# Signs of the routed rows made one slot later on ScalarE, and VectorE's convolutions ahead of the scores, in the last ten slots of a gated delta layer

## The reference

```python
    x = x + _L0_attn_b_ref(_layernorm(x), ...)     # gated delta
    x = x + _L0_ffn_ref(_layernorm(x), ...)        # routed splines
...
        q = _silu(_dwconv_causal(x @ Wq, conv_q_w, conv_q_b))   # k, v alike
        alpha = sigmoid(x @ Wa + ba); beta = sigmoid(x @ Wb + bb)
        # scan over t:
                err = einsum('bhvk,bhk->bhv', S, kt) - vt
                S = at * S - bt * err * kt
                o = einsum('bhvk,bhk->bhv', S, qt)
        o = (o - mu) * rsqrt(var + 1e-05) * ln_w + ln_b
        o = (o * sigmoid(x @ Wg)) @ Wo
...
            # routed splines, xf = layer-normed rows
            input_sigs = sign(xf)
            cluster_scores = input_sigs @ cluster_sigs.T
            best_cluster = argmax(cluster_scores)
            tile_scores = input_sigs @ tile_sigs.T
            tile_idx = argmax(where(in_cluster, tile_scores, -inf))
```

## Time and profile before

| what | value |
|---|---|
| median of 3 runs | 3161.95 us |
| the profiled execution's own time | 3159.97 us |
| its span | 3158.2 us |
| slots 64 to 73 (from the first `carried` of slot 64, 2759.86, to the end of the last residual, 3073.37) | 313.51 us |
| of it busy: VectorE, TensorE, GpSimd, ScalarE | 258.92, 215.15, 173.11, 157.06 us |
| granted TensorE clock, mean of slots 64, 65, 66, 67, 68 | 0.88, 0.84, 0.84, 0.87, 0.84 |
| the same, slots 69, 70, 71, 72, 73 | 0.97, 0.94, 1.00, 0.87, 0.56 |
| behind them, to the end of the span | 84.83 us |

### The profile page before, as it was taken

The page is one execution under the profiler, slowest core; times in us unless marked ns, Lnnn a source line. Parts: engine busy times, 40 slices in busy tenths (PEclk is TensorE's granted clock), DMA queues, the critical chain, the costliest instruction groups (busy, mean ns, idle before and its releaser), DMA issues.

```text
span 3158.2 us, 65711 instructions
## 1 busy us (share of the span) xinstructions
PE 2652.7 (84%) x21856; PEld 2161.5 (68%) x21872; DVE 2253.1 (71%) x5574; ACT 2146.7 (68%) x5247; POOL 2029.7 (64%) x2171
## 2 busy tenths in 40 slices
PE   6889889646579999999999999999999999877753
PEld 3555555425458788887878888788787888756642
DVE  5777778575457776776767767667677677679876
ACT  4767776424358777878878778788787787755631
POOL 3544554333667778787786877868768787676442
PEclk9999999667789999999999999999999999988975
DMA  2000000014577676776767666676776767633311
GB/s 98 0 0 0 0 0 0 3 55 108 137 188 206 159 203 153 193 195 160 202 155 193 191 172 180 175 190 179 178 185 177 194 162 192 163 84 99 82 28 53
DMA packets 750315, 402.08 MB, mean 127 GB/s; under 512 B 406867, under 2 KB 686163, under 8 KB 749910
## 3 DMA queue, kind: packets, MB, share of 16 engines
q1 hardware_dynamic: 750038, 398.59, 48.4%
HBM read 263.80 MB, written 134.62 MB: 126 GB/s over the span
## 4 chain that ended last, share of the span: by engine, by line
PE 40%; DVE 16%; POOL 15%; issue 14%; ACT 12%; DMA 1%; SPq 1%; POOLq 0%; DVEq 0%; ACTq 0%
PE bank L2051 16%; PE bank L2219 7%; PE bank L2102 4%; ACT acc L1116 3%; POOL outer L877 3%; PE bank L2082 3%; POOL ors L890 3%; POOL prob L776 2%; POOL inv L880 2%; ACT shifted L1114 2%; DVE acc L1646 2%; POOL acc L863 2%; POOL oT L896 2%; PE bank L2167 2%; DVE ostat L1705 2%
## 5 line engine op out<-in xcount | busy, mean ns | idle before, releaser
L863 POOL TENSOR_TENSOR acc<-acc,shifted 128x510 f32<-128x510 f32 x384 | 585.0, 1524 | 460.6 <-DVE acc L1646 458.7
L1646 DVE SCALAR_TENSOR_TENSOR acc<-bank,conv_w,acc 128x254 f32<-128x254 f32 (+1 forms) x1536 | 630.1, 471 | 190.1 <-ACT acc L1116 189.5
L2051 PE MATMUL bank<-x_k,w_kq 128*128 128x256 f32 x2048 | 507.8, 398 | 25.3 <-DMA x_k<-xT_scratch 25.3
L1114 ACT ACTIVATE shifted<-bank,conv_w 128x255 f32<-128x255 f32 x768 | 366.0, 476 | 136.7 <-issue 66.9
L2051 PEld LDWEIGHTS bank<-x_k,w_kq 128*128 128x128 f32 x2048 | 387.4, 196 | 90.0 <-DMA x_k<-xT_scratch 15.2
L1116 ACT ACTIVATE acc<-bank,conv_b,conv_w 128x256 f32<-128x256 f32 x768 | 438.5, 571 | 0.0
L776 POOL TENSOR_TENSOR prob<-prob,rinv 128x512 f32<-128x512 f32 x192 | 201.8, 1054 | 266.3 <-DVE rinv L1442 266.1
L2219 PE MATMUL bank<-w_o,oT 128*128 128x256 f32 x1024 | 249.4, 389 | 80.8 <-POOL oT L896 79.2
L880 POOL TENSOR_TENSOR inv<-inv,outer 128x30 f32<-128x30 f32 (+14 forms) x480 | 285.8, 595 | 37.6
L877 POOL TENSOR_TENSOR outer<-inv 128x30 f32<-128x30 f32 (+14 forms) x480 | 264.8, 552 | 35.9 <-DMA inv<-D_scratch 7.9
L2219 PEld LDWEIGHTS bank<-w_o,oT 128*128 128x128 f32 x1024 | 188.4, 193 | 122.8 <-issue 99.3
(11 more groups left out here) (243 smaller groups left out, 5849.8 us busy)
## 6 DMA issues: line engine op xcount, KB each, us to landing
abc<-decay_scratch SPq DMA_DIRECT2D x64, 512.0 KB, 5.2
MTm<-M_scratch SPq DMA_DIRECT2D x128, 256.0 KB, 3.4
kqm<-q_scratch SPq DMA_DIRECT2D x64, 512.0 KB, 4.9
knm<-k_scratch SPq DMA_DIRECT2D x64, 258.0 KB, 4.0
x_k<-xT_scratch SPq DMA_DIRECT2D x64, 256.0 KB, 2.9
q_scratch<-kq SPq DMA_DIRECT2D x128, 128.0 KB, 3.1
q_scratch<-kq SPq DMA_DIRECT2D x64, 256.0 KB, 3.6
D_scratch<-LM SPq DMA_DIRECT2D x256, 64.0 KB
```

The lines of the kernel that those rows point to most:

```text
L863: pool.tensor_tensor(dst, dst, shifted[:, u % 2, :, 1:], ALU.add).then_inc(Z["sumk" if u < 4 else "sumv"], 1)
L1114: act.activation(shifted[:, u % 2, i % 2, 1:], pj[:, 0:SEQ - 1], ACT.Copy, scale=conv_w[:, kind, bass.ds(head, 1), TAPS - 2:TAPS - 1].rear ...
L1646: dve.scalar_tensor_tensor(out=acc[:, kind, i, t:], in0=pj[:, 0:SEQ - t], scalar=wcol, in1=acc[:, kind, i, t:], op0=ALU.mult, op1=ALU.add) ...
L2051: mm = pe.matmul(dst[:, i * SEQ:(i + 1) * SEQ], w[:, k, head * DK:(head + 1) * DK], x[:, k, :], start=(k == 0), stop=(k == CT - 1))
```

## The change

ScalarE makes the signs of a slot's unit in the next slot, behind `joined("x")` and ahead of `gate(0)`, and no longer as the last thing of the slot itself. Those of slot 73 are made behind the last slot together with those of 74, which is where they stood. VectorE's list runs conv(4), conv(5), weighted, scores, second_out, spread instead of conv(4), scores, conv(5), second_out, weighted, spread. Nothing is added or removed, and no wait is edited.

```diff
@@ block.scalar, slot(s)
-                rt = drained(s)
+                old = drained(s - 1)
...
                     if joining(s):
                         joined("x")
+                    if old:
+                        signs(tiles1, old[0], old[2])
                     if h is not None:
                         gate(0)
...
                     if h is not None:
                         from_state()
-                    if rt:
-                        signs(tiles1, rt[0], rt[2])
...
-            g, b, w = drained(STEPS + LAG_N)
-            signs(tiles1, g, w)
+            for s in (STEPS + LAG_N - 1, STEPS + LAG_N):
+                g, b, w = drained(s)
+                signs(tiles1, g, w)
@@ block.vector, slot(s)
                     if f is not None:
-                        conv(4)
-                    routed(3)
-                    if f is not None:
-                        conv(5)
-                    if n is not None:
-                        second_out()
+                        conv(4), conv(5)
                     if h is not None:
                         weighted()
+                    routed(3)
                     if n is not None:
-                        spread(), moments_of_out()
+                        second_out(), spread(), moments_of_out()
```

## The result

The changed kernel takes 3153.93 us (median of 9 runs, 3148.21 to 3158.05), the kernel before 3161.36 beside it (9 runs, 3158.54 to 3165.29): a ratio of 0.9974, with a 95% interval of 0.9964 to 0.9984. In microseconds that is 7.4 gained, 5 to 11 by the interval. The forecast was 3154.5, faster by 7.4 us.

A forecast was written before the change was run, and what follows sets the result against it. VectorE was taken to bound the next `carried` in slots 64 to 73 once `upper` is free. 4.67 + 0.65 + 4.3 - 0.3 + 0.6 - 2.0 - 0.5 - 0.25 + 0.2 = 7.4 us gained: 3154.5, range 3150 to 3160.5.

The forecast's parts named there:

- tails: From a slot's `spread` to the next `carried`: VectorE idles there vanish, 4.67 us in slots 65 to 68, 0.65 in 69.
- wide fronts: From `carried` to `spread` in slots 66 to 69: 10.0 us each, 4.3 gained, less 0.3 in slot 66.
- The step that TensorE gets ahead: Turn of slot 68 to 69: with `upper` free earlier, TensorE leads VectorE by about 3.6 us, so `carried` needn't wait.
- GpSimd was taken at 0.2 a slot: Wide slots: VectorE operations waiting for GpSimd's scales cost 0.2 us a slot, out of a possible 0 to 1.0.
- the tail of slots 64 and 69 to 71: Between `spread` and the next `carried`: no loss; +0.65 us in slot 69, and `spread` 0.6 earlier in slot 64.
- narrow fronts: From `carried` to `spread` in slots 70 and 71: 1.0 us lost in each, -2.0 together, bounds -1.1 and -2.2.
- Slower: Rival, chance 0.07: TensorE not ahead, signs on the chain in every slot, wide fronts 13.1, 11 us lost, 3173.
- Held back: Rival, chance 0.18: sign product waits for GpSimd's power or `add_shifted(5)`, TensorE cools; gain 3.2 us, 3158.8.
- Nothing: Rival, chance 0.08: something hidden, `project_out` or a load, bounds the wide slots' tails; 2.7 us gained, 3159.
- Slot 73 and what follows: Slot 73 loses about 0.25 us and gains 0.2 at its start; what follows is in the same order.
- the forecast case: Outcome with a gain of 5 to 9 us, chance 0.53; about five sevenths of it measurably faster.
- faster: Sign of the whole-kernel time: less than 3155.6 us, given chance 0.58 as 0.14 + 0.44.

The follow-up runs named there:

- signs_only: Changed kernel, but with VectorE's order of the kernel before; only ScalarE's signs are moved: 3172.43 us, ratio 1.0037 to the kernel before.
- order_only: Changed kernel, but with the signs left last in ScalarE's slot; only VectorE's list is new: 3172.83 us, ratio 1.0028 to the kernel before.
- wide_state_early: Changed kernel, but slots 64 and 70 to 73 in the order of before, except `weighted` ahead of `second_out`: 3151.57 us timed, ratio 0.9965 to the kernel before.
- state_late: Changed kernel, but with `weighted` behind `second_out` in every slot: 3156.81 us in one run, 3160.52 for the kernel before beside it.
- wide_only: Changed kernel, but slots 64 and 70 to 73 keep the order of the kernel before: 3153.78 us, ratio 0.9973 to the kernel before.
- early_signs: Against `wide_only`, signs of the wide units stand behind `tap(5)`, ahead of `lower`: 3151.09 us, ratio 0.997 to the kernel before.

## Why the prediction was right, and where it was off

**The bound and the tails held.** The idles ahead of `carried` were what the tail could give. Slots 67 and 68 gave 1.10 and 1.90 (forecast 1.15 and 1.93), slot 66 0.20 instead of 0.60: its power starts 2.87 us behind `spread` where it was 2.59, and 0.3 had been taken off for that. Slot 65 gave 1.48 (0.99): its front grew by 2.28 and its tail shrank by 3.76, GpSimd setting the point in between.

**The wide fronts held**: 10.12, 10.14, 9.73 and 9.69 for a forecast of 10.0, worth 4.66 us in slots 66 to 69 against 4.3 less 0.3. The step that TensorE gets ahead is shown three times: by the rows of the turn, by `signs_only`, which has it and the short tails, and by `order_only`, which lacks both. GpSimd was taken at 0.2 a slot. In slots 66 to 69 it is GpSimd that pays. Slot 68 after the change:

```profile
2903.36 1.72 POOL L744 TENSOR_TENSOR frs<-fvar,half_neg 128x4 f32<-128x4 f32 x1
2905.16 1.11 POOL L749 TENSOR_TENSOR fvar<-frs 128x4 f32<-128x4 f32 x1
```

against 1.02 and 0.20 alone: the power runs beside `weighted` (2903.53, 0.68 long) and the next scale beside the sign product (2904.99), and both VectorE operations keep their own length. The scale began 0.17 behind the product and waited, as the forecast had it. The Trainium skill (SBUF — State Buffer, "SBUF: two separate sides") has an exclusive lock, by which the later of the two waits; the scale agrees. The power doesn't: by its row it began 0.17 ahead of `weighted` and is longer by `weighted`'s length all the same, in slots 66, 67 and 68 alike. Why GpSimd loses there, no run shows; that the rows of GpSimd start too early is possible.

**The term that failed is the tail of slots 64 and 69 to 71.** The forecast put nothing there ("TensorE's own `second_out` needs some 1.2 ... and hides") except +0.65 in slot 69 and +0.6 in slot 64; it never asked what `weighted` ahead sets off on TensorE. The state came earlier, nobody needed it earlier, and the idle that had been in pieces became one piece ahead of `outT`, after which the granted clock was 0.52. Slot 64's front won 0.31 and its tail lost 0.92: -0.61 instead of +0.6. That one is not sure to come: `order_only` and the second execution of `wide_state_early` have the same order there and an idle of 3.73 ahead of `outT`, where the changed kernel has 3.72, and still an `outT` of 1.11 and 1.09 and tails of 18.86. Slot 69's tail is 0.46 longer instead of 0.65 shorter; `state_late` and `signs_only`, with `weighted` late, have the 18.9 that the forecast worked out. Slots 70 and 71 lose 0.66 and 0.64. `second_rhs` waits 1.69 longer there; about 0.94 of it comes back, since VectorE used to wait that long for `project_out` later in slot 70 and now doesn't. In all 3.3 us of the forecast's sum. In slots 66 to 68 the clock fell too, at no price:

```profile
2915.24 1.97 PE L2206 MATMUL bank<-ident,o 128*128 128x128 f32 x8 [5.66 <-DVE o L1722]
```

This is `outT` of slot 68, 1.04 long before the change. But `second_rhs` waits for TensorE in none of these three slots, as VectorE's parts for four tiles lie ahead of it, and the tails came out as forecast.

**The narrow fronts were right in kind, not in size.** Slot 70 paid 0.11, slot 71 1.59, for -1.0 in each slot. In slot 70 a premise was wrong: TensorE is ahead there too, `carried` starts without the idle of 1.04 that it had, and TT's copy ends at C + 6.17 instead of C + 6.71. In slot 71 `carried` waits as before, and the collision with `add_shifted(5)` that was priced "up to 0.5" costs 0.94:

```profile
2998.17 1.26 POOL L863 TENSOR_TENSOR acc<-acc,shifted 128x510 f32<-128x510 f32 x1
...
2998.35 1.63 DVE L1361 TENSOR_TENSOR sgn<-sgn,sl_sign 128x512 f32<-128x512 f32 x1 [0.98 <-ACT sgn L991]
```

In slot 71 the product starts 0.18 behind the addition and takes 1.63; in slot 70 it takes 0.69:

```profile
2968.10 0.69 DVE L1361 TENSOR_TENSOR sgn<-sgn,sl_sign 128x512 f32<-128x512 f32 x1 [0.98 <-ACT sgn L991]
```

Without it slot 71's front would have paid 0.65, where the forecast's own sum had 0.6. The price depends on how much of the addition is left: in `state_late` it starts 0.73 ahead of the product in slots 70 and 71, and the product takes 1.09 and 1.08. Slot 72 took +0.52 for +0.3.

**The rivals.** "Slower" did not happen; `order_only`, where TensorE isn't ahead either, shows wide fronts as long as it feared, by another path. "Held back" happened in one slot of nine, as the product in slot 71. "Nothing" fell: no load and no `project_out` stands behind the idles of the wide slots.

**The total.** The drain of the traces gained 5.4 us, the medians say 7.4 and, repeated, 6.3, with an interval of 3 to 11. So the traces bear out less than the forecast's sum, and that the median hit it to 0.6 us is partly luck. Slot 73 and what follows was 0.69 shorter instead of 0.25 longer. That is TensorE's clock in `project_out` of slot 73, before and after:

```profile
3066.68 5.96 PE L2219 MATMUL bank<-w_o,oT 128*128 128x256 f32 x16 [1.60 <-POOL oT L896]
```

```profile
3064.99 5.31 PE L2216 MATMUL bank<-w_o,oT 128*128 128x256 f32 x16 [1.61 <-POOL oT L896]
```

The granted clock is 0.61 in the first and 0.69 in the second. In the twelve profiles the stretch from slot 73 on is 107.0 to 107.5 us where this product takes 5.1 to 5.4, and 108.1 to 108.6 where it takes 6.0 to 6.2; the two executions of `wide_state_early`, one kernel, are one of each. So this gain too is outside the forecast's mechanism.

**A slip in the chances.** Five sevenths of the forecast case's 0.53 are 0.38, not 0.44, so that "faster" had 0.52 by the forecast's own terms.

## What to carry to other kernels

An instruction that waits in an in-order list is best judged by who stands behind it; moving it pays only if the other engines' lists are changed so that they have work until its new time, and each half of such a change can lose while both together win. An operation moved ahead "because it is free" (here `weighted`) should be followed on the engine that consumes it: work that is done early leaves an idle in one piece later, and TensorE may come out of that at half its clock. Collisions between VectorE and GpSimd should be costed per place, by what is left of the operation that is in the way, and not as a mean.

## What the hardware showed that I had not expected

**TensorE behind an idle.** In slots 64 and 69 to 71 the chain `outT` and `keys_on_state` took 1.09 and 1.95 us at a granted clock of 1.00 before the change and 1.97 and 3.3 to 3.6 at 0.50 to 0.53 after it. Ahead of the fast ones stood idles of 1.77, 2.55, 2.64 and 3.44 us, ahead of the slow ones 3.72, 5.75, 6.58 and 6.68. But the idle just ahead does not decide alone. Slots 71 and 72 of the kernel before:

```profile
3011.61 1.09 PE L2209 MATMUL bank<-ident,o 128*128 128x128 f32 x8 [3.44 <-DVE o L1721]
...
3038.05 1.97 PE L2209 MATMUL bank<-ident,o 128*128 128x128 f32 x8 [3.42 <-DVE o L1721]
```

And in `wide_only`, with the order of before in slot 71, `outT` took 1.48 behind the same 3.44. In slots 69 to 71 of the changed kernel the clock is back behind `keys_on_state`: the transposes that follow took 1.07.

**What a collision costs.** `normalise` took 3.01 us behind the start of GpSimd's pick and 1.22 where it began ahead of the pick, the sign product 1.63 for 0.69 and, in `order_only`, 2.29 for 1.21. GpSimd's power took 1.72 for 1.02, and in `early_signs`, with `weighted` and the sign product on VectorE one behind the other, 2.86:

```profile
2830.63 2.86 POOL L749 TENSOR_TENSOR frs<-fvar,half_neg 128x4 f32<-128x4 f32 x1
```

**How far executions differ.** With the same instructions up to there, slot 64 began between 2758.4 and 2765.1 us in the twelve profiles. Differences of that size between single spans say nothing of a change of 5 us. Slots compared one by one do, if TensorE's clock in them is compared too.
